# Wide one-hots of the edge counting in a graph network: four tensor_scalar instructions in place of one tensor_tensor

## The chip, the cores and the metric

The kernel runs on one core of a Trainium2 chip. Five engines work side by side: PE (TensorE, matrix products), DVE (VectorE), ACT (ScalarE), POOL (GpSimd) and SP (SyncE, which issues DMAs here). They meet through semaphores. The metric is the device time of one execution in microseconds; lower is better.

## What is computed

Four graph layers over 6250 nodes and 100000 edges (sorted by target node), each with a residual and a layer normalization: attention with 8 heads and a feed-forward part, attention with 4 heads and a gated skip, four rounds of graph convolution, two rounds of sum aggregation with two-layer networks. The two attentions, cut down:

```
score = einsum('ehd,ehd->eh', K[src], Q[dst]) / sqrt(D_HEAD)
s     = exp(clip(score, -5.0, 5.0))[:, :, None]
wV    = segment_sum(V[src] * s, dst);  z = segment_sum(s, dst)         # layer 0
score = einsum('ehc,ehc->eh', q[dst], k[src]) / sqrt(OUT_C)            # layer 1
alpha = softmax of score over the edges of one dst;  out = segment_sum(v[src] * alpha, dst)
```

The later layers need only sums over neighbours. They multiply with a dense matrix of counts, how many edges lead from one node to another, as bytes in device memory. That matrix is made beside the two attentions.

## The kernel before

**The sweeps.** Two sweeps go over the edges in steps of 128 edges, one edge on each partition, all with one target block of 128 nodes. Four steps (HALF = 4) are a half turn; a sweep has 208 half turns. `attend` is the first sweep (layer 0), `score` the second (layer 1).

**POOL** does nothing but gathers in both (`gathers4`, L544): for each step one indirect DMA that fetches keys and values of 128 source nodes. Four to a half turn, 832 to a sweep, into a ring of 8 buffers (`ring4`), each guarded by a semaphore that is waited for before the first gather of a half turn.

**DVE** has the longest list. In a half turn of the first sweep: the message product L788 of the half turn before, then a piece of the counting (`count_lo`, L289, and `count_place`, L295), the product of gathered keys with queries L769 (it waits for the gather), `hits16` L556, the reduction L776, then L781 (clip) and the sums L751 and L321 in turn. In the second: `count_lo`, an L321, `count_place`, L321, `hits16` L556, L321, the product L962 (it waits for the gather), L321 and the reduction L966.

**The counting.** A group is four steps of it. For each step DVE makes two one-hot matrices, both with the edges on the partitions: `by_lo` (128 columns: the source node within its block) and `by_place` (WIDE = 392 columns: source block and place of the target in a window of 8 nodes). PE multiplies them (`count_product`, L331) to a 128x392 block of counts in PSUM, ACT turns it to bytes (`count_move`, L340), DVE adds it to a ring of slots (`count_add`, L321), and SP stores finished slots. The first sweep makes a group in two half turns: a quarter of `by_place` and `by_lo` in the odd one, three quarters in the even one. The second makes one in each half turn and two in 6 of 16 half turns.

The four steps of a group lie innermost in both one-hots: `by_place` is [2, WIDE, HALF], and a source tile `count_fours` of [WIDE, HALF] float16 holds each column's number four times. One tensor_tensor compares it with the four numbers of the group, repeated along the columns. So PE reads the columns of one step 8 bytes apart. `hits16` and `count_lo` use the first 128 columns of `count_fours` in the same way.

DVE's instructions and waits are in the order in which the code writes them; nothing reorders them.

Of the kernel before, what the change touches and what calls it, by code (L numbers as in the profile page):

```python
# [24 lines left out]
P = 128  # L25
# [7 lines left out]
HALF = 4  # L33
# [24 lines left out]
BF16 = mybir.dt.bfloat16  # L58
# [3 lines left out]
F16 = mybir.dt.float16  # L62
# [177 lines left out]
class Counting:  # L240


    def __init__(self, nc, ctx):
        def sb(name, n, dt=F32):
            return ctx.enter_context(nc.sbuf_tensor(name, [P, n], dt))

        def split(t, *shape):
            names = " ".join("abc"[:len(shape)])
            return t[:, :].rearrange(f"p ({names}) -> p {names}", **dict(zip("abc", shape)))

        self.lo, self.place = sb("count_lo", WCOLS, F16), sb("count_place", WCOLS, F16)
        self.tables = sb("count_tables", WCOLS, I32)
        self.fours = split(sb("count_fours", HALF * WIDE, F16), WIDE, HALF)
        self.by_lo = split(sb("by_lo", 2 * HALF * P, BF16), 2, P, HALF)
        self.by_place = split(sb("by_place", 2 * HALF * WIDE, BF16), 2, WIDE, HALF)
# [36 lines left out]
def count_place(dve, ct, c, r, first=0, last=WIDE):  # L292

    n = slice(first, last)
    return dve.tensor_tensor(ct.by_place[:, r % 2, n], ct.fours[:, n], copies(ct.place[:, ds(c * HALF, HALF)], 1, last - first),  # L295
                             ALU.is_equal)
# [28 lines left out]
def count_product(pe, m, ct, c, r, k, bank, banks):  # L325


    if k == 0:
        pe.wait_ge(ct.hot, c + 1)
    wait(pe, ct.moved, c * HALF + k - banks + 1)  # L330
    pe.matmul(m.bank(bank, WIDE), ct.by_lo[:, r % 2, :, k], ct.by_place[:, r % 2, :, k], start=True, stop=True).then_inc(ct.product, 1)  # L331
# [284 lines left out]
def attend(nc, m, ct, adj, table):  # L616
# [4 lines left out]
    with Phase(nc, "at0", "used added hit_ready turned copied q_ready multiplied "  # L621
# [105 lines left out]
        def _(dve):  # L727
# [10 lines left out]
            def half(i, j, h, r, c, first=False):  # L738
# [18 lines left out]
                if odd:  # L757
                    count_lo(dve, ct, c + 1, r // 2 + 1)
                    count_place(dve, ct, c + 1, r // 2 + 1, 0, WIDE // 4)
                    ct.load_of(dve, count_regs[r // 2 % 2], c)  # L760
                    count_stored(dve, ct, c, r // 2)
                else:
                    count_place(dve, ct, c, r // 2, WIDE // 4, WIDE).then_inc(ct.hot, 1)
                    ct.load_to(dve, count_regs[r // 2 % 2], c)
# [30 lines left out]
            count_place(dve, ct, 0, 0, 0, WIDE // 4)  # L795
# [8 lines left out]
            count_place(dve, ct, AT_GROUPS, AT_GROUPS, WIDE // 4, WIDE).then_inc(ct.hot, 1)  # L804
# [1090 lines left out]
def plan_windows(nc, m, ct, t, table):  # L1895


    with Phase(nc, "pw", "rows_in made vec compared counted picked drawn taken loaded0 loaded1 projected copied stored0 stored1") as (
# [48 lines left out]
        def _(dve):  # L1947
# [16 lines left out]
            then(dve.tensor_copy(ct.fours, copies(m.wramp[:, 0:WIDE], 2, HALF)))  # L1964
# [948 lines left out]
```

## Time and profile before

| | |
|---|---|
| median of 3 runs | 5402.13 us |
| lowest, highest | 5399.48, 5411.69 us |
| the profiled execution | 5400.67 us |
| its span, first to last instruction | 5398.3 us |
| mean granted clock of TensorE | 0.885 |
| PE busy | 4350.4 us, 81% |
| DVE busy | 3580.8 us, 66% |
| POOL busy | 2766.0 us, 51% |
| ACT busy | 2266.3 us, 42% |

Busy times are sums over stages that have different limits, so a share of the whole span says little of any one stage. Times in the rows below are microseconds from the start of the span, unless marked as nanoseconds. An instruction of DVE may start some 0.08 us before the recorded end of the one ahead of it, since its start overlaps the other's end.

### The profile page before, as it was taken

How to read it: one execution, taken by the hardware profiler on the slowest of the kernel's cores; microseconds unless marked ns; L12 is line 12 of the kernel's file. 1: busy time of each engine (PE TensorE's matmuls, PEld its weight loads, DVE VectorE, ACT ScalarE, POOL GpSimd, SP SyncE). 2: the span in 40 equal slices, each digit the busy share in tenths (PEclk: the TensorE clock that was granted, in tenths of full speed). 3: DMA queues.
4: the chain of work that ended last, by engine and by line, in shares of the span. 5: the costliest groups of instructions: out<-in, count | busy, mean ns of one | idle time of the engine just before them, and what ended most of it. 6: DMA issues, size and time to landing. Idle time of an engine off the chain costs nothing. (4 is left out here: it accounts for less than half of the span.)

```text
span 5398.3 us, 99723 instructions
## 1 busy us (share of the span) xinstructions
PE 4350.4 (81%) x24072; PEld 3655.1 (68%) x24073; DVE 3580.8 (66%) x7929; ACT 2266.3 (42%) x4134; POOL 2766.0 (51%) x2730
## 2 busy tenths in 40 slices
PE   7566666766767777777468849999999999999998
PEld 4455555554344444444257639999999999999998
DVE  4888888888778888888776674444445654444444
ACT  0333434343245555555246644444444443344333
POOL 0477777774077777777221104444444443344433
PEclk8788888888977787777789959999999999999999
DMA  1444444443267777777235434343444443233332
GB/s 41 124 117 117 118 117 117 116 118 99 96 182 198 200 200 197 203 201 202 70 111 157 136 114 152 132 154 145 149 155 156 174 141 118 96 144 138 133 126 95
DMA packets 543103, 750.01 MB, mean 139 GB/s; under 512 B 57967, under 2 KB 441966, under 8 KB 542734
## 3 DMA queue, kind: packets, MB, share of 16 engines
q1 hardware_dynamic: 461182, 521.35, 28.8%
q0 software_dynamic: 81552, 224.63, 15.5%
q8 instruction: 123, 2.02, 0.1%
q14 instruction: 246, 2.02, 0.1%
HBM read 584.36 MB, written 161.41 MB: 138 GB/s over the span
## 5 line engine op out<-in xcount | busy, mean ns | idle before, releaser
L544 POOL DMA_INDIRECT arena<-table_kv,arena x1664 | 1721.9, 1035 | 653.5 <-issue 506.4
L2350 PE MATMUL ps<-moving,parts 128*128 128x384 f32 (+1 forms) x11662 | 2015.3, 331 | 36.3 <-ACT moving L2412 20.4
L2350 PEld LDWEIGHTS ps<-moving,parts 128*128 128x128 f32 x11662 | 1948.7, 188 | 70.1 <-ACT moving L2412 29.4
L2291 POOL CAST moving<-counts 128x1152 fp32r<-128x1152 uint8 (+1 forms) x420 | 476.7, 1135 | 736.8 <-PE ps L2350 604.7
L340 ACT ACTIVATE counted<-ps 128x392 uint8<-128x392 f32 x1568 | 665.0, 502 | 324.5 <-PE ps L331 283.7
L2291 POOL CAST moving<-big 128x1152 fp32r<-128x1152 uint8 (+1 forms) x413 | 468.4, 1134 | 608.6 <-PE ps L2350 608.6
L331 PE MATMUL ps<-by_place,by_lo 128*128 128x392 bf16 x1568 | 631.3, 525 | 101.9 <-DVE by_place L295 95.5
L654 PE MATMUL ps<-arena 128*128 128x137 f32 x1664 | 325.2, 352 | 338.1 <-DVE arena L788 322.3
L2412 ACT ACTIVATE moving<-counts 128x1152 fp32r<-128x1152 uint8 (+1 forms) x360 | 366.9, 1024 | 436.5 <-PE ps L2350 433.6
L2412 ACT ACTIVATE moving<-big 128x1152 fp32r<-128x1152 uint8 (+1 forms) x354 | 360.4, 1023 | 429.2 <-PE ps L2350 429.0
L654 PEld LDWEIGHTS ps<-arena 128*128 128x128 f32 x1664 | 276.8, 242 | 367.6 <-ACT arena L699 217.6
L2557 DVE CAST moving<-counts 128x1152 fp32r<-128x1152 uint8 (+1 forms) x240 | 312.8, 1303 | 287.2 <-PE ps L2350 287.2
L2557 DVE CAST moving<-big 128x1152 fp32r<-128x1152 uint8 (+1 forms) x236 | 307.5, 1303 | 288.8 <-PE ps L2350 288.8
L562 PEld LDWEIGHTS ps<-arena 128*128 128x128 bf16 x1680 | 141.6, 123 | 523.5 <-DVE arena L556 450.8
L321 DVE TENSOR_TENSOR slots<-slots,counted 128x196 uint16 x1568 | 406.6, 259 | 89.1 <-DVE slots L321 43.0
L562 PE MATMUL ps<-arena 128*128 128x128 bf16 x1680 | 199.6, 252 | 271.5 <-DVE arena L556 269.0
L295 DVE TENSOR_TENSOR by_place<-count_fours,count_place 128x1568 bf16<-128x1568 f16 (+1 forms) x497 | 395.6, 796 | 0.0
L331 PEld LDWEIGHTS ps<-by_place,by_lo 128*128 128x128 bf16 x1568 | 187.7, 123 | 249.2 <-issue 179.2
L883 PE MATMUL ps<-big,arena 128*128 x1672 | 313.5, 348 | 0.4 <-ACT arena L909 0.4
L883 PEld LDWEIGHTS ps<-big,arena 128*128 128x128 f32 x1672 | 292.3, 257 | 27.9 <-issue 18.6
L666 PE MATMUL ps<-big,arena 128*128 x1680 | 288.9, 330 | 0.4 <-ACT arena L694 0.4
L704 ACT ACTIVATE arena<-arena 128x32 f32<-128x32 f32 x208 | 48.3, 232 | 571.5 <-DVE arena L781 571.5
(329 smaller groups left out, 5311.9 us busy)
## 6 DMA issues: line engine op xcount, KB each, us to landing
counts<-adjacency SPq DMA_DIRECT2D x53, 2352.0 KB, 8.6
big<-adjacency SPq DMA_DIRECT2D x52, 2352.0 KB, 8.5
adjacency<-slots SPq DMA_DIRECT2D x784, 98.0 KB
edge_values<-arena SPq DMA_DIRECT2D x208, 256.0 KB, 3.3
arena<-edge_values SPq DMA_DIRECT2D x208, 256.0 KB, 3.2
arena<-table_kv,arena POOLq DMA_INDIRECT x1664
big<-table_norm SPq DMA_DIRECT2D x60, 192.0 KB, 5.6
big<-adjacency SPq DMA_DIRECT2D x7, 1568.0 KB, 6.5
```

What stands on the lines that cost most here:

```text
L295: return dve.tensor_tensor(ct.by_place[:, r % 2, n], ct.fours[:, n], copies(ct.place[:, ds(c * HALF, HALF)], 1, last - first), ALU.is_equal)
L321: dve.tensor_tensor(ct.slot_pairs[:, ds(to[k], WIDE // 2)], ct.slot_pairs[:, ds(of[k], WIDE // 2)], ct.counted_pairs[:, r % 2, k, :], ALU. ...
L331: pe.matmul(m.bank(bank, WIDE), ct.by_lo[:, r % 2, :, k], ct.by_place[:, r % 2, :, k], start=True, stop=True).then_inc(ct.product, 1)
L340: act.activation(ct.counted[:, r % 2, k, :], m.bank(bank, WIDE), ACT.Copy).then_inc(ct.moved, 1)
L544: pool.indirect_dma_start(m.ring4[r][:, k * 2 * D:(k + 1) * 2 * D], None, table, bass.IndirectOffsetOnAxis(m.src[:, j * HALF + k:j * HALF ...
L562: mm = pe.matmul(bank[:, k * P:(k + 1) * P], m.hit16[:, r, :, k], m.ident16, start=True, stop=True)
L654: mm = pe.matmul(summed(k), m.hit[:, r % 2, k, :], m.msg[:, r % 2, k, :], start=True, stop=True)
L883: mm = pe.matmul(m.bank(6 + h)[:, k * P:(k + 1) * P], m.hitT[:, h, k, :], m.q[:, ds(at[k] * D, D)], start=True, stop=True)
L2291: pool.tensor_copy(to, of).then_inc(by_pool, 1)
L2350: mm = pe.matmul(m.bank(g % 2, n * P), d.parts[SOURCE[u]][:, s + q, t_, :], moving[:, q * n * P:(q + 1) * n * P], start=(s + q == 0 and t_ ...
L2412: act.activation(to, of, ACT.Copy).then_inc(by_act, 1)
L2557: dve.tensor_copy(to, of).then_inc(by_dve, 1)
```

## The change

`by_place` is now [2, HALF, WIDE]: a step's 392 columns lie together. It is made a step at a time: a row of the numbers 0 to 391 (`count_iota`, float16) is compared with one number per partition, a tensor_scalar with the operand `ct.place[:, step]`, which is now float32. A group takes four such instructions in place of one (second sweep) or two (first sweep, which now splits them one and three). `count_fours` shrinks to 128 columns. PE reads the columns of a step contiguously.

```diff
-        self.lo, self.place = sb("count_lo", WCOLS, F16), sb("count_place", WCOLS, F16)
+        self.lo, self.place = sb("count_lo", WCOLS, F16), sb("count_place", WCOLS)
-        self.fours = split(sb("count_fours", HALF * WIDE, F16), WIDE, HALF)
+        self.fours = split(sb("count_fours", HALF * P, F16), P, HALF)
+        self.iota = sb("count_iota", WIDE, F16)
-        self.by_place = split(sb("by_place", 2 * HALF * WIDE, BF16), 2, WIDE, HALF)
+        self.by_place = split(sb("by_place", 2 * HALF * WIDE, BF16), 2, HALF, WIDE)
...
-def count_place(dve, ct, c, r, first=0, last=WIDE):
-
-    n = slice(first, last)
-    return dve.tensor_tensor(ct.by_place[:, r % 2, n], ct.fours[:, n], copies(ct.place[:, ds(c * HALF, HALF)], 1, last - first),
-                             ALU.is_equal)
+def count_place(dve, ct, c, r, steps=range(HALF)):
+
+    for k in steps:
+        op = dve.tensor_scalar(ct.by_place[:, r % 2, k, :], ct.iota[:, :], ct.place[:, ds(c * HALF + k, 1)], None, ALU.is_equal)
+    return op
...
-    pe.matmul(m.bank(bank, WIDE), ct.by_lo[:, r % 2, :, k], ct.by_place[:, r % 2, :, k], start=True, stop=True).then_inc(ct.product, 1)
+    pe.matmul(m.bank(bank, WIDE), ct.by_lo[:, r % 2, :, k], ct.by_place[:, r % 2, k, :], start=True, stop=True).then_inc(ct.product, 1)
...
-                    count_place(dve, ct, c + 1, r // 2 + 1, 0, WIDE // 4)
+                    count_place(dve, ct, c + 1, r // 2 + 1, range(1))
...
-                    count_place(dve, ct, c, r // 2, WIDE // 4, WIDE).then_inc(ct.hot, 1)
+                    count_place(dve, ct, c, r // 2, range(1, HALF)).then_inc(ct.hot, 1)
...
-            then(dve.tensor_copy(ct.fours, copies(m.wramp[:, 0:WIDE], 2, HALF)))
+            then(dve.tensor_copy(ct.fours, copies(m.wramp[:, 0:P], 2, HALF)))
+            then(dve.tensor_copy(ct.iota[:, :], m.wramp[:, 0:WIDE]))
```

The order of DVE's instructions in an even half turn of the first sweep, from the message product to the product with the queries; ISA and REGISTER_ALU are the register computations for the operand behind them. Before:

```order
L788 TENSOR_TENSOR arena<-arena 128x4x128
L295 TENSOR_TENSOR by_place<-count_fours,count_place 128x1176
L267 ISA
L267 TENSOR_LOAD count_tables
L275 ISA x2
L769 TENSOR_TENSOR arena<-arena,ps 128x512
```

And after the change, the same place (line numbers are one higher than before):

```order
L789 TENSOR_TENSOR arena<-arena 128x4x128
L296 ISA
L296 TENSOR_SCALAR by_place<-count_iota,count_place 128x392
L296 ISA
L296 TENSOR_SCALAR by_place<-count_iota,count_place 128x392
L296 ISA
L296 TENSOR_SCALAR by_place<-count_iota,count_place 128x392
L268 REGISTER_ALU
L268 TENSOR_LOAD count_tables
L276 ISA x2
L770 TENSOR_TENSOR arena<-arena,ps 128x512
```

One instruction of 1176 elements has become three of 392, right behind the message product; nothing else has moved. In the second sweep, from `count_lo` to the next load of table entries, DVE's order after the change:

```order
L290 TENSOR_TENSOR by_lo<-count_fours,count_lo 128x512
L322 ISA
L322 TENSOR_TENSOR slots<-slots,counted 128x196
L296 ISA
L296 TENSOR_SCALAR by_place<-count_iota,count_place 128x392
L296 ISA
L296 TENSOR_SCALAR by_place<-count_iota,count_place 128x392
L296 ISA
L296 TENSOR_SCALAR by_place<-count_iota,count_place 128x392
L296 ISA
L296 TENSOR_SCALAR by_place<-count_iota,count_place 128x392
L268 REGISTER_ALU
```

Before, one instruction of 128x1568 stood where the four stand.

## Rows read from the trace of the kernel before

**Rows 1.** Busy time by stretch: microseconds, each engine, granted clock, DMA share, GB/s.
```profile
190.00:1320.00 1130.00, 780.12 (x4606) 646.09 (x4605) 976.55 (x2609) 442.62 (x1044) 854.70 (x830) 0.84 0.40 116
1490.00:2620.00 1130.00, 796.85 (x3645) 475.05 (x3643) 928.87 (x2348) 595.27 (x1359) 860.85 (x829) 0.77 0.71 197
3220.00:5398.00 2178.00, 2140.07 (x12603) 2084.79 (x12603) 1037.11 (x1616) 876.40 (x1050) 944.09 (x833) 1.00 0.38 138
```

**Rows 2.** First sweep by shape: busy us, mean ns of one, idle before it.
```profile
L544 POOL DMA_INDIRECT arena<-table_kv,arena x830 | 855.2, 1030 | 252.9 <-issue 252.9
L788 DVE TENSOR_TENSOR arena<-arena 128x512 f32<-128x512 f32 x208 | 143.2, 689 | 0.3 <-ACT arena L704 0.3
L556 DVE TENSOR_TENSOR arena<-count_fours,arena 128x512 bf16<-128x512 f16 x208 | 89.1, 428 | 27.0 <-issue 4.2
L295 DVE TENSOR_TENSOR by_place<-count_fours,count_place 128x1176 bf16<-128x1176 f16 x105 | 80.2, 764 | 0.0
L289 DVE TENSOR_TENSOR by_lo<-count_fours,count_lo 128x512 bf16<-128x512 f16 x104 | 43.5, 418 | 0.0
L295 DVE TENSOR_TENSOR by_place<-count_fours,count_place 128x392 bf16<-128x392 f16 x104 | 37.1, 357 | 0.0
```

**Rows 3.** Second sweep by shape.
```profile
L544 POOL DMA_INDIRECT arena<-table_kv,arena x829 | 861.3, 1039 | 252.6 <-issue 252.6
L331 PE MATMUL ps<-by_place,by_lo 128*128 128x392 bf16 x1149 | 450.4, 527 | 97.8 <-DVE by_place L295 92.0 <-issue 4.2
L321 DVE TENSOR_TENSOR slots<-slots,counted 128x196 uint16 x1152 | 296.1, 257 | 84.4 <-DVE slots L321 42.8 <-issue 20.3 <-ACT counted L340 14.8
L295 DVE TENSOR_TENSOR by_place<-count_fours,count_place 128x1568 bf16<-128x1568 f16 x286 | 277.0, 968 | 0.0
L289 DVE TENSOR_TENSOR by_lo<-count_fours,count_lo 128x512 bf16<-128x512 f16 x286 | 120.5, 421 | 35.0 <-issue 20.5 <-PE ps L331 13.4
L556 DVE TENSOR_TENSOR arena<-count_fours,arena 128x512 bf16<-128x512 f16 x207 | 87.9, 425 | 0.0
```

**Rows 4.** Waits of DVE, first sweep, then second: us, times, longest.
```profile
DVE arena L769 <- DMA arena<-table_kv,arena: 101.9, 180, 1.5
...
DVE arena L962 <- DMA arena<-table_kv,arena: 75.2, 59, 5.2
```

**Rows 5.** Durations of the gathers, second sweep, shortest, median, longest.
```profile
L544 POOL DMA_INDIRECT arena<-table_kv,arena x829: 942/947/2379, 1489.5 to 2602.2; - x166
```

**Rows 6.** Timeline of the second sweep: a gather behind L295.
```profile
2012.93 0.97 DVE L295 TENSOR_TENSOR by_place<-count_fours,count_place 128x1568 bf16<-128x1568 f16 x1
2013.12 1.59 POOL L544 DMA_INDIRECT arena<-table_kv,arena  x1 [0.30 <-issue]
```

**Rows 7.** Timeline of the first sweep: a gather behind L788.
```profile
709.78 0.69 DVE L788 TENSOR_TENSOR arena<-arena 128x512 f32<-128x512 f32 x1
710.06 1.23 POOL L544 DMA_INDIRECT arena<-table_kv,arena  x1 [0.30 <-issue]
710.39 0.42 DVE L289 TENSOR_TENSOR by_lo<-count_fours,count_lo 128x512 bf16<-128x512 f16 x1
```

**Rows 8.** Timeline of the first sweep: L781 in a gather; then all L781.
```profile
707.56 0.94 POOL L544 DMA_INDIRECT arena<-table_kv,arena  x1 [0.30 <-issue]
708.19 0.32 DVE L781 TENSOR_SCALAR arena<-arena 128x32 f32<-128x32 f32 x1
...
L781 DVE TENSOR_SCALAR arena<-arena x208: 167/175/386, 197.7 to 1302.0; 128x32 f32<-128x32 f32 x104
```

**Rows 9.** Timeline of the planning: DVE instructions with a number per partition.
```profile
10.10 1.28 DVE L472 TENSOR_SCALAR arena<-arena,small 128x896 f32<-128x896 f32 x2
...
26.54 0.28 DVE L482 TENSOR_SCALAR arena<-arena,tile_id 128x128 f32<-128x128 f32 x1
26.74 0.28 DVE L484 TENSOR_SCALAR arena<-arena,tile_id 128x128 f32<-128x128 f32 x1
```

**Rows 10.** Costliest groups of the page: the dense part's product.
```profile
L2350 PE MATMUL ps<-moving,parts 128*128 128x384 f32 (+1 forms) x11662 | 2015.3, 331 | 36.3 <-ACT moving L2412 20.4
```

More of the change, by code:

```diff
@@ L794, in _ @@
             count_lo(dve, ct, 0, 0)
-            count_place(dve, ct, 0, 0, 0, WIDE // 4)
+            count_place(dve, ct, 0, 0, range(1))
             dve.memset(m.sums[:, 0:BLOCKS * A0], 0.0).then_inc(ones_in, 1)
@@ L803, in _ @@
                     half(i, RINGS * i + r, r % 2, r, RINGS // 2 * i + r // 2)
-            count_place(dve, ct, AT_GROUPS, AT_GROUPS, WIDE // 4, WIDE).then_inc(ct.hot, 1)
+            count_place(dve, ct, AT_GROUPS, AT_GROUPS, range(1, HALF)).then_inc(ct.hot, 1)
             to_count, of_count = ct.at(dve, count_regs[(AT_GROUPS - 1) % 2])
```

## The prediction

> **What bounds the kernel now.** I read the windows first [rows 1]. The program has three long stretches: the first sweep (190 to 1320 us), the second (1490 to 2620 us) and the dense part after 3220 us. The last has PE busy 2140 of 2178 us and runs none of the changed code, so the question lies in the two sweeps. In neither is PE, ACT or DVE full: DVE is busy 977 and 929 of 1130 us.
>
> The groups of each sweep by shape [rows 2, 3] settle it. POOL issues 4 indirect gathers a half turn, 832 in a sweep. Its only idle time in either sweep is "issue", 252.9 and 252.6 us, 0.305 us ahead of each gather: it never waits for a ring buffer, for DVE or for a transfer. 855.2 + 252.9 = 1108 us is the first sweep, 861.3 + 252.6 = 1114 us the second. DVE waits for what POOL fetched, 101.9 us at L769 in the first and 75.2 us at L962 in the second [rows 4]. So **a sweep lasts as long as POOL's gathers, and DVE has 102 and 75 us to spare**. A change on DVE counts by what it does to the time of a gather, until DVE has used its slack up.
>
> Next, what makes a gather long. The shortest is 942 ns and the median 947, but the longest 2379 [rows 5] and the means are 1030 and 1039 [rows 2, 3]. Against 0.944 us each the excess is 855.2 - 830 x 0.944 = 71.7 us in the first sweep and 861.3 - 829 x 0.944 = 78.7 us in the second. The timeline shows the cause. In [rows 6] L295 runs from 2012.93 to 2013.90; the gather that starts at 2013.12 takes 1.59 us and ends 0.81 us after L295. In [rows 7] L788 ends at 710.47 and the gather ends at 711.29, 0.82 us later. An undisturbed gather needs 0.944 us, so both look as if they had started 0.13 us ahead of the end of the DVE instruction. Both DVE instructions read two tensors in SBUF. **First hold:** a gather that starts while such an instruction runs waits for it, to 0.13 us before its recorded end.
>
> The other direction is in [rows 8]. L781, a tensor_scalar with one SBUF source, starts 0.63 us into a gather and ends with it, at 708.51, in place of taking its median 175 ns: it got going at +0.78 us. Its longest is 386 ns, 0.21 above the median, so it is held from +0.57 us at the latest. **Second hold:** from +0.57 to +0.78 us a gather keeps a tensor_scalar of this sort waiting. Nothing here shows whether a tensor_scalar that is already running makes the gather wait at +0.57; L781, with 32 elements, is too short.
>
> **The change, part by part.** L295 goes, by_place is filled by tensor_scalar of 392 elements, four in a group. 104 or 105 groups are made in the first sweep, 286 in the second.
>
> *Length of one new instruction.* L482 and L484, also with a number per partition, start 0.195 us apart at 128 float32 elements and last 0.28; two L472 of 896 take 1.28 us, which with the same overlap of 0.08 is 0.60 apart [rows 9]. That is 0.53 ns an element and 0.13 us fixed. The new source and result are 2 bytes wide. No row has a one-source instruction of that kind, but two-source ones show what width does: L788, 512 float32, 689 ns; L289, 512 of 2 bytes, 418 ns [rows 2]: 0.53 ns an element less, half the rate of 1.06. I take the same halving: 392 x 0.265 + 0.13 = 0.23 us apart, 0.315 long. If the width bought nothing it is 392 x 0.53 + 0.13 = 0.34; at one element a cycle, as L788, 0.54.
>
> *DVE's work.* Second sweep: L295 took 0.968 - 0.08 = 0.885 us of DVE's time, four new ones take 0.93: +0.04 x 286 = +12 us. First sweep: 0.68 + 0.27 = 0.95 a group before, 0.93 after: nothing. Each new instruction has a register computation of its own ahead of it (the rows of the order above), 4 where there was 1; short beside 0.23, and I cost it at nothing.
>
> The Trainium skill (VectorE: DVE Perf Modes, section "The perf-mode tier table") lets tensor_scalar on 2-byte SBUF operands stream at four elements a cycle, tensor_tensor at two. The halving above agrees with it. By that rule alone a group would stream 1568 elements in 0.41 us in place of 0.82, and DVE would win 117 us in the second sweep; by the rows three more fixed parts of 0.13 us take all of that back.
>
> *DVE held by POOL.* The four run 0.93 us and are held if one wants to start in the second hold, 0.21 us in each 1.31 us: chance (0.93 + 0.21) / 1.31 = 0.87, mean wait half of 0.21: 0.09 x 286 = 26 us in the second sweep and 10 in the first. Together +38 of the 75 us of slack in the second; the first has 102.
>
> *POOL, first hold, second sweep.* A hold of length h hits starts in proportion to h and then costs h/2, so shares go by h squared, h being the duration less 0.13 us: L295 0.84^2 x 286 = 202, L289 24, L556 18, L321 19, in all 263. L295's share of 78.7 us is 60 us. The new ones: 0.185^2 x 1144 = 39, that is 12 us. This is the gain: -48 us.
> *Second hold, second sweep.* If a running tensor_scalar delays POOL at +0.57 as it does at the start, another 12 us; if it keeps POOL to its recorded end, 0.315^2 x 1144 = 114 or 34 us; if not at all, 0. I take 18, between the first two. **Second sweep: -60 + 12 + 18 = -30 us, bounds -48 and -14.** DVE allows 75 - 38 = 37 us of it, so it is barely covered, and -37 is the most unless DVE's own waits shrink. They may, a little: the 392-column product has mean 527 ns with columns 8 bytes apart, against 331 for 384 columns at L2350 [rows 3, 10]; its columns now lie together. That is not counted.
>
> *First sweep.* By the same squares L295 would own 48 of 140, 24 us. But it stands right behind L788, on which the gather waits first; the next starts 1.25 us later, when L295 is over. I take 5 of the 24; 2 come back from the new ones. New is this: after L788 ends at E, the gather's second hold falls at E + 0.44. In even half turns three new instructions start at E - 0.08, + 0.15 and + 0.38; the third would hold to E + 0.565. 104 x 0.125 = 13 us if POOL waits for it; to its recorded end, with the one of odd half turns too, 40; 0 if not at all. **First sweep: -5 + 2 + 13 = +10 us, bounds -17 and +37.**
>
> *Preparation.* One copy shrinks by 1056 elements and one of 392 is added, once: under 1 us.
>
> Sum: -30 + 10 = **-20 us**. The profiled execution took 5400.67 us, span 5398.3, 1.5 us under the median of 5402.13. 5400.67 - 20 = 5380.7; I say **5381 us**.
>
> **The rivals.**
> *A, the pair stays locked (slower).* If back-to-back tensor_scalars never let POOL in between, each group holds as one block of 3 x 0.23 + 0.185 = 0.88 us: 65 us at the first hold and 65 at the second, +70 in the second sweep; in the first, +25. 5400.67 + 95 = **5496 us**. It decides from the point where more than two in a row keep the hold. Against it: in [rows 7] L289 stood ready behind L788, started at 710.39 before L788's end, and POOL still got in at L788's end. For it: those only read through the contested side, and a tensor_scalar may also take the writing side. The Trainium skill (SBUF — State Buffer, section "SBUF: two separate sides") warns that a Vector instruction in a two-port mode keeps GpSimd from writing its descriptors, with tensor_copy as the example; L781's row agrees that the two exclude each other, in the opposite order. 10 in 100.
> *B, the width buys nothing (slower).* 0.34 us apart: 1.34 a group, +0.45 x 286 = +130 us in the second sweep, plus 26 held, against 75 of slack: +81. The first sweep absorbs 0.19 x 208 = 40. DVE becomes the bound of the second sweep: **5480 us**. 8 in 100, with the one-element rate (5700 us and more) in it.
> *C, nothing to see.* The two holds give back what the one took; the gathers keep their mean of 1.03 to 1.04: **5401 us**. 17 in 100.
> *D, the second hold never waits for DVE.* -48, capped by DVE at about -40 with faster products, and -3 in the first sweep: **5358 us**. 20 in 100.
> The forecast has the remaining 45.
>
> **The numbers.** Forecast and own range: 5381, 5350 to 5405. A measurement tells 0.2%, 11 us, from no change. Faster: all of D and three quarters of the forecast, with a little of C, 0.56. Same: most of C and a tenth of the forecast, 0.20. Slower: A, B, and the sixth of the forecast in which the first sweep goes to its upper bound, 0.24. The range that leaves out 2 in 10 runs from 5345 to 5450; A and B lie beyond.
>
> **What the profile would show.** Right: L296 at about 0.315 us, starts 0.23 apart; L544 still with "issue" as its only idle time, its mean down to about 1.00 in the second sweep and up to 1.04 in the first; the wait at L962 down to some 10 us. Wrong: L296 at 0.42 or more (B); L544 above 1.08 (A); a sweep in which DVE no longer waits for gathers, where POOL's gain is lost.

## The result, and the profile after

| | before | after |
|---|---|---|
| median | 5406.55 us | 5418.13 us |
| lowest, highest (20 executions each) | 5395.16, 5415.69 | 5407.31, 5424.99 |
| the profiled execution | 5400.67 us | 5417.27 us |
| its span | 5398.3 us | 5415.2 us |

The ratio is 1.0021, 95% interval 1.0014 to 1.0028: **slower by 0.2%**, 12 us, where 20 us less was forecast. It is a small number, but the experiments below show that it is the difference of two larger ones. (The changed kernel was measured once more with the first experiments, as twice_after, and stood 18 us above the kernel before beside it.)

The windows of the kernel after, columns as in [rows 1]:

```profile
190.00:1320.00 1130.00, 732.96 (x4613) 639.50 (x4614) 979.71 (x2825) 442.77 (x1045) 850.31 (x828) 0.84 0.41 116
1490.00:2620.00 1130.00, 676.00 (x3595) 485.96 (x3596) 940.60 (x3161) 583.88 (x1334) 805.61 (x825) 0.75 0.70 195
3220.00:5398.00 2178.00, 2135.78 (x12569) 2081.32 (x12569) 1040.18 (x1625) 878.10 (x1050) 946.85 (x833) 0.99 0.38 140
```

In the second sweep POOL's busy time fell from 861 to 806 us in the same 1130 us, and yet it issued 825 gathers in place of 829. Something else now sets the pace. The granted clock of TensorE there is 0.75 after 0.77, and PE is busy 676 of 1130 us: it bounds nothing. The groups of that sweep by shape, columns as in [rows 3]:

```profile
L545 POOL DMA_INDIRECT arena<-table_kv,arena x825 | 805.6, 977 | 296.8 <-issue 238.5 <-SPq L859 58.3
L332 PE MATMUL ps<-by_place,by_lo 128*128 128x392 bf16 x1128 | 315.9, 416 | 114.2 <-DVE by_place L296 112.3 <-issue 0.6
L296 DVE TENSOR_SCALAR by_place<-count_iota,count_place 128x392 bf16<-128x392 f16 x1132 | 298.0, 324 | 0.0
L322 DVE TENSOR_TENSOR slots<-slots,counted 128x196 uint16 x1130 | 291.1, 258 | 141.2 <-issue 63.1 <-DVE slots L322 38.9 <-ACT counted L341 36.1
L963 DVE TENSOR_TENSOR arena<-arena,ps 128x512 f32<-128x512 f32 x206 | 140.4, 682 | 11.4 <-DMA arena<-table_kv,arena 7.9 <-issue 1.7 <-PE ps L884 1.4
L290 DVE TENSOR_TENSOR by_lo<-count_fours,count_lo 128x512 bf16<-128x512 f16 x282 | 118.6, 421 | 34.7 <-issue 31.6 <-PE ps L332 1.2
```

A gather takes 977 ns, not 1039. But POOL, which never waited before, now waits 58.3 us. Its releaser is SP's L859, the line after which a ring buffer is free; the buffer is full of rows that DVE has not yet used, since DVE's own wait for gathers has shrunk from 75.2 to 7.9 us (L963). **DVE has become the bound of the second sweep.** And it has done so less by working than by standing still: ahead of L322 it is idle 141.2 us, of which "issue" is 63.1. It was 84.4 with 20.3.

From its first gather to its last L322 (L321 before) the second sweep took 1485.5 to 2618.3 before, 1132.8 us, and takes 1481.1 to 2635.6 after, 1154.5 us: **+21.7**. The first sweep is 2.4 us shorter, and its two groups are unchanged in what they say, with POOL idle for "issue" alone and DVE still with time to spare:

```profile
L545 POOL DMA_INDIRECT arena<-table_kv,arena x828 | 850.9, 1028 | 252.4 <-issue 252.4
L770 DVE TENSOR_TENSOR arena<-arena,ps 128x512 f32<-128x512 f32 x208 | 143.1, 688 | 102.5 <-DMA arena<-table_kv,arena 102.4
L296 DVE TENSOR_SCALAR by_place<-count_iota,count_place 128x392 bf16<-128x392 f16 x419 | 134.7, 364 | 0.0
```

Where does DVE stand idle in the second sweep? The timeline of DVE shows one half turn (start and duration in us, in brackets the idle time ahead and its cause):

```profile
1997.08 1.04 DVE L296 TENSOR_SCALAR by_place<-count_iota,count_place 128x392 bf16<-128x392 f16 x4
1998.17 0.26 DVE L322 TENSOR_TENSOR slots<-slots,counted 128x196 uint16 x1
1998.35 0.43 DVE L557 TENSOR_TENSOR arena<-count_fours,arena 128x512 bf16<-128x512 f16 x1
1999.32 0.26 DVE L322 TENSOR_TENSOR slots<-slots,counted 128x196 uint16 x1 [0.54 <-issue]
```

The gap lies between `hits16` (L557) and the next `count_add`; over the sweep it has a mean of 0.46 us, and had 0.18 before (worked out from the starts in the two traces). In the code `ct.load_of` stands at that place: DVE's sequencer loads four slot numbers from a table in SBUF into registers (L272). The L322 behind it doesn't use them. They go into the set `following` and are used by the next group's L322. But it stands behind the load in DVE's list, and after this load the L322 starts 0.23 us or more after the load's end, in every half turn of the trace after. Three views of single lines show what the sequencers did at this moment (min/median/max ns, then the times; DVEq and SPq are the sequencers of DVE and SP):

```profile
L347 SPq TENSOR_LOAD <-count_tables x1: 300/300/300, 1998.0 to 1998.0; - x1
L348 SPq TENSOR_LOAD <-count_tables x1: 626/626/626, 1998.4 to 1998.4; - x1
L272 DVEq TENSOR_LOAD <-count_tables x1: 611/611/611, 1998.5 to 1998.5; - x1
```

SP loads its own table entries for `count_store` (L347, L348), and its second load overlaps DVE's. The first of SP's two takes 0.30 us; here the second and DVE's both take over 0.61. Over the sweep, the kernel after first, then the kernel before:

```profile
L272 DVEq TENSOR_LOAD <-count_tables x283: 337/510/944, 1490.4 to 2618.6; - x142
```

```profile
L271 DVEq TENSOR_LOAD <-count_tables x287: 336/345/876, 1494.8 to 2616.0; - x144
```

The median load of DVE went from 345 to 510 ns. Counting overlaps in the trace, 38 of 283 loads met one of SP's before and 170 of 278 after (mean 0.62 us for those, 0.40 for the rest). It is SP's second load that goes with the long ones: of the 160 loads L272 that met L348, 130 took 0.5 us or more, and of the other 128 of the sweep 19; the 15 beside L347 alone have a median of 345 ns. An overlap doesn't explain every long load, though: in the kernel before, SP's second load met no load of DVE's 207 times and still took 0.5 us or more in 101 of them. So two causes stood to be told apart: the load *starts* late, since the four L296 each bring a register computation of 57 ns to the same sequencer, or the load *takes* long, since it now meets SP's.

### The profile page after: what moved, and what is told of

The parts are those of the page before. It is cut to its first block and busy times, and to the rows that moved or that the text cites. A ratio compares the mean times of both kernels' runs of the same rounds, so it can differ in the third digit from the quotient of the medians.

```text
span 5415.2 us, 100831 instructions
## 1 busy us (share of the span) xinstructions
PE 4189.2 (77%) x24072; PEld 3665.1 (68%) x24073; DVE 3607.2 (67%) x9001; ACT 2264.6 (42%) x4134; POOL 2714.0 (50%) x2730
## 5 line engine op out<-in xcount | busy, mean ns | idle before, releaser
L545 POOL DMA_INDIRECT arena<-table_kv,arena x1664 | 1667.3, 1002 | 698.8 <-issue 493.6
L2414 ACT ACTIVATE moving<-big 128x1152 fp32r<-128x1152 uint8 (+1 forms) x354 | 360.3, 1023 | 430.6 <-PE ps L2352 430.4
L332 PE MATMUL ps<-by_place,by_lo 128*128 128x392 bf16 x1568 | 441.8, 404 | 123.9 <-DVE by_place L296 121.9
L322 DVE TENSOR_TENSOR slots<-slots,counted 128x196 uint16 x1568 | 406.5, 259 | 148.0 <-issue 63.1
L296 DVE TENSOR_SCALAR by_place<-count_iota,count_place 128x392 bf16<-128x392 f16 x1568 | 437.3, 335 | 0.0
L884 PE MATMUL ps<-big,arena 128*128 x1672 | 331.4, 362 | 0.4 <-ACT arena L910 0.4
L884 PEld LDWEIGHTS ps<-big,arena 128*128 128x128 f32 x1672 | 305.5, 269 | 6.5 <-issue 2.9
L667 PE MATMUL ps<-big,arena 128*128 x1680 | 292.0, 332 | 0.4 <-ACT arena L695 0.4
```

What stands on the lines that cost most here:

```text
L296: op = dve.tensor_scalar(ct.by_place[:, r % 2, k, :], ct.iota[:, :], ct.place[:, ds(c * HALF + k, 1)], None, ALU.is_equal)
L322: dve.tensor_tensor(ct.slot_pairs[:, ds(to[k], WIDE // 2)], ct.slot_pairs[:, ds(of[k], WIDE // 2)], ct.counted_pairs[:, r % 2, k, :], ALU. ...
L545: pool.indirect_dma_start(m.ring4[r][:, k * 2 * D:(k + 1) * 2 * D], None, table, bass.IndirectOffsetOnAxis(m.src[:, j * HALF + k:j * HALF ...
L884: mm = pe.matmul(m.bank(6 + h)[:, k * P:(k + 1) * P], m.hitT[:, h, k, :], m.q[:, ds(at[k] * D, D)], start=True, stop=True)
L2414: act.activation(to, of, ACT.Copy).then_inc(by_act, 1)
```

## The experiments

The theory at the start: **T** (theory S in the expectations), POOL's side went as forecast or better, and DVE lost the gain at the uncovered load. Rivals: **R1**, the gathers cost DVE more than they did (second hold), and **R2**, four short instructions are simply more work for DVE (R1 and R2 together are theory W); **P**, the chain from the product through ACT to L322 sets the pace. **R3** was formed after these: the load is late by the register computations alone, or long by a collision with SP (theory C). Ratios are to the kernel before, measured beside each (medians 5398.25 with late_after, late_before, twice_after and four_tt; 5402.08 with split_after, one_ts, static_after and late_four_tt; 5395.76 with the three that move SP's loads). In two kernels, one_ts and static_after, part of the one-hots is replaced as told there; the counts are then other ones, the program takes a long branch behind the dense part that the others don't (13388.32 and 13384.19 us in all), and only their sweeps are read.

**late_after.** The load moves to a place where DVE's engine has 0.68 us of work in hand:

```diff
                     hits16(dve, m, ct, (r + 2) % 4, (j + 2) * HALF).then_inc(hit_ready, 1)
-                    ct.load_of(dve, following, c)
                     count(2)
...
                                       m.bank(6 + r % 2).rearrange("p (k n) -> p k n", k=HALF), ALU.mult).then_inc(multiplied, 1)
+                    ct.load_of(dve, following, c)
                     count(3)
```

> The changed kernel, with the second sweep's load of the four source offsets (L272) moved from behind hits16 (L557) to behind the product L963, ahead of the last L322. Theory S (the sequencer of DVE): after the change DVE's queue is filled with short instructions, its sequencer runs less far ahead, and the load stands uncovered between L557 and the next L322 (idle 0.46 us a single group against 0.18 before). Behind a product of 0.6 us it is covered again: that idle falls to 0.2 us or less, about 0.25 us x 206 = 50 us come free on DVE, POOL becomes the bound of the second sweep again at (0.98 + 0.305) x 832 = 1070 us, DVE waits for gathers at L963 again, and the kernel is some 35 to 50 us faster than the changed one: 5365 to 5385 us. Theory W (DVE's added work and its being held by POOL fill the sweep, wherever the load stands): nothing or under 10 us is gained, the idle time turns up at another instruction. Theory P (the chain from product to ACT to L322 sets the pace): the same as W, with L322 waiting for ACT.

5352.17 us, ratio 0.9906 (0.9891 to 0.9921). The changed kernel measured beside it (twice_after, below) took 5416.68, so the move is worth 64 us; the second sweep is 64.3 us shorter (1090.2). That is more than the 35 to 50 expected. The groups of its second sweep:

```profile
L545 POOL DMA_INDIRECT arena<-table_kv,arena x823 | 802.6, 975 | 250.8 <-issue 247.4 <-SPq L859 3.4
L322 DVE TENSOR_TENSOR slots<-slots,counted 128x196 uint16 x1149 | 295.0, 257 | 94.8 <-DVE slots L322 39.5 <-issue 38.8 <-ACT counted L341 8.4
L962 DVE TENSOR_TENSOR arena<-arena,ps 128x512 f32<-128x512 f32 x207 | 140.4, 678 | 12.6 <-DMA arena<-table_kv,arena 11.3 <-issue 1.1
```

and its DVE timeline, where the gap behind L557 is gone and 0.17 us are left behind the product:

```profile
2003.77 0.25 DVE L322 TENSOR_TENSOR slots<-slots,counted 128x196 uint16 x1
2003.94 0.41 DVE L557 TENSOR_TENSOR arena<-count_fours,arena 128x512 bf16<-128x512 f16 x1
2004.47 0.26 DVE L322 TENSOR_TENSOR slots<-slots,counted 128x196 uint16 x1
2004.65 0.68 DVE L962 TENSOR_TENSOR arena<-arena,ps 128x512 f32<-128x512 f32 x1
2005.50 0.26 DVE L322 TENSOR_TENSOR slots<-slots,counted 128x196 uint16 x1 [0.17 <-issue]
```

POOL's mean is the same 975 as with the change alone (977), its wait for the ring is gone, and the time with it. T holds. R1, R2 and P fall as the main cause: the edit touches neither DVE's work nor the order of the chain through ACT, the gathers are as long as with the change, and the time came back.

**late_before.** The same move in the kernel before.

> The kernel before with the same load moved in the same way. Theory S: before the change POOL bounds the second sweep, so DVE's time is free and nothing moves: within 0.2% of before (5400 to 5412 us), gathers with mean 1.03 to 1.05 us. If the load's place by itself were worth the time whatever the counting does, this kernel would gain as many microseconds as the changed one gains from it.

5384.5 us, ratio 0.9965 (0.9952 to 0.9978). A small gain where none was expected: POOL never waited there, but its gathers went from 1039 to 1023 ns. The groups of its second sweep:

```profile
L544 POOL DMA_INDIRECT arena<-table_kv,arena x829 | 847.7, 1023 | 252.7 <-issue 252.4 <-SPq L858 0.3
L321 DVE TENSOR_TENSOR slots<-slots,counted 128x196 uint16 x1152 | 294.0, 255 | 71.9 <-DVE slots L321 39.5 <-issue 13.3 <-ACT counted L340 8.1
```

That what DVE does earlier or later shifts which of its two-source instructions a gather meets is a guess that no run tests. Against the same kernel before, the change alone gives +18 us (twice_after) and the move alone -14, and together they give -46: the move is worth 14 us without the change and 64 with it.

**twice_after.** A second, identical `ct.load_of` behind the first, to double the suspected cost.

> The changed kernel with the load L272 issued twice in each single group of the second sweep (the same values into the same registers). Theory S: the load is on DVE's path there, so a second one costs nearly all its length, 0.35 to 0.5 us x 206 = 70 to 105 us: 5490 to 5525 us. Theories W and P: it is hidden behind the waits that are there anyhow, under 20 us.

5416.68 us, 1.0028 (1.0019 to 1.0038). The trace has 392 loads L272, as the trace of the change has, not more: the build merged the two, and this is the changed kernel once more. It tells nothing of the theory; it repeats the measurement of the change, beside late_after.

**split_after.** The doubling done in a way that the build keeps:

```diff
-                    ct.load_of(dve, following, c)
+                    dve.load(following[HALF:HALF + 2], ct.tables[32:33, ds(c * HALF, 2)])
+                    dve.load(following[HALF + 2:], ct.tables[32:33, ds(c * HALF + 2, 2)])
```

> The changed kernel with the load L272 of each single group in the second sweep cut in two loads of two values each, at the same place, behind hits16 (L557). It is the real form of the doubled load: two identical loads were merged into one when the kernel was built, so that run was the changed kernel again. Theory S (the load stands uncovered on DVE's sequencer ahead of an L322): the idle time ahead of that L322 grows from 0.46 us by nearly a load, 0.35 us or more, a single group takes 4.6 us or more in place of 4.29, and the second sweep is 55 to 100 us longer than the changed kernel's: 5470 to 5515 us. Theories W and P (work and holds, or the product chain, set the pace): under 20 us.

5603.21 us, 1.0374 (1.036 to 1.0387): in the expected direction and twice as far (187 us in the second sweep, where 55 to 100 was expected). The second sweep takes 1341.8 us. Its groups by shape, and then the two loads by their lines:

```profile
L545 POOL DMA_INDIRECT arena<-table_kv,arena x731 | 700.0, 958 | 430.9 <-SPq L859 245.0 <-issue 185.9
L322 DVE TENSOR_TENSOR slots<-slots,counted 128x196 uint16 x970 | 249.1, 257 | 281.6 <-issue 227.2 <-DVE slots L322 39.1 <-ACT counted L341 14.4
```

```profile
L958 DVEq TENSOR_LOAD <-count_tables x176: 528/959/1142, 1492.2 to 2615.6; - x176
L959 DVEq TENSOR_LOAD <-count_tables x176: 524/528/1172, 1492.8 to 2616.6; - x176
```

Two loads of two values are far dearer than one of four: at least 0.52 us each, with a median of 0.96 for the first. POOL's gathers are the shortest of all (958), and it waits 245 us. DVE's sequencer alone can make the sweep 18% longer than before (1341.8 / 1132.8).

**four_tt.** The other way round: the kernel before with `count_place` of the second sweep in four tensor_tensors of 392, without the change's layout.

```diff
-                    count_place(dve, ct, c + 1, p + 1).then_inc(ct.hot, 1)
+                    for n4 in range(4):
+                        placed = count_place(dve, ct, c + 1, p + 1, n4 * (WIDE // 4), (n4 + 1) * (WIDE // 4))
+                    placed.then_inc(ct.hot, 1)
```

> The kernel before with the second sweep's wide compare cut in four tensor_tensor instructions of 392 elements, one behind the other; the kind of instruction, the layout and PE's strided columns stay as before. If it is the length of one uninterrupted instruction that makes gathers long (first hold), the gathers of the second sweep fall from a mean of 1.039 to about 0.98 to 1.00 us, as with the change, though these are the same two-tensor instructions. If it is their kind or their sum of busy time, the mean stays at 1.03 or above. For the time: four instructions stand 0.27 us apart, 1.10 us a group against 0.89, 60 us more work for DVE, and by theory S the loads lose their cover too: slower than before by 30 to 90 us (5435 to 5495 us). By theory W alone (work minus the 75 us of slack) about 5400 to 5410 us.

5408.3 us, 1.0015 (1.0005 to 1.0024). The groups of its second sweep:

```profile
L544 POOL DMA_INDIRECT arena<-table_kv,arena x828 | 831.1, 1004 | 264.6 <-issue 246.3 <-SPq L858 18.3
L321 DVE TENSOR_TENSOR slots<-slots,counted 128x196 uint16 x1140 | 292.1, 256 | 98.7 <-DVE slots L321 37.6 <-issue 29.2 <-ACT counted L340 28.6
```

By theory S 5435 to 5495 us was expected here, by theory W 5400 to 5410: the time came out as W says, so this run by itself speaks for the rival. It shows how much of the picture comes from the cutting alone: gathers down from 1039 to 1004 of the change's 977, the wait for the ring begun (18.3 us), the median load up to 469 ns. But the load is not late: it starts 0.61 us ahead of the end of `hits16` (medians here and below, from the traces), against 0.53 in the kernel before and 0.37 in the kernel after. four_tt has one register computation a group. The rest of the change's picture goes with the kind of the instruction, the four computations and the layout together; no run separates the kind from the layout.

**late_four_tt.** four_tt with the load moved.

> The kernel before with the second sweep's compare in four tensor_tensor instructions and the load moved behind the product. It has both parts of the moved changed kernel (short holds, covered load) but not the kind of instruction nor the contiguous columns. Theory: POOL bounds the sweep again, gathers of mean 1.00 as without the move, (1.00 + 0.305) x 832 = 1086 us against 1118 before: 25 to 35 us faster than before, 5365 to 5380 us, 10 to 25 us behind the moved changed kernel, since its DVE has 0.13 us a group more work and its gathers wait a little longer. If the kind or the layout matters by itself, it stays near before, 5390 us or more.

5395.95 us, 0.9989 (0.9981 to 0.9998), where 5365 to 5380 was expected. The ring's wait went (3.0 us), but the gathers went back to 1034 ns, the longest to 2848 ns: POOL is the bound again, with DVE waiting 39.6 us for it. late_after, with tensor_scalars and the new layout, keeps them at 975. So cutting and a covered load are not enough for its gain; whether the kind of the instruction or the layout gives the rest was not tried apart.

**static_after.** The number per partition is always that of the first group, at a fixed place, so that DVE's sequencer has nothing to compute. The one-hots of all later groups are thus left out.

```diff
-        op = dve.tensor_scalar(ct.by_place[:, r % 2, k, :], ct.iota[:, :], ct.place[:, ds(c * HALF + k, 1)], None, ALU.is_equal)
+        op = dve.tensor_scalar(ct.by_place[:, r % 2, k, :], ct.iota[:, :], ct.place[:, k:k + 1], None, ALU.is_equal)
```

> The changed kernel with the number per partition read at a fixed place, the first four columns, in all groups: no register computation stands ahead of any tensor_scalar. The output is not the reference's: every group's wide one-hots are those of the first four steps. If it is the register computations (four where there was one) that put the sequencer behind, the idle ahead of L322 falls from 0.46 to about 0.2 us and the kernel gains 30 to 60 us on the changed one: 5360 to 5385 us. If it is that short instructions fill the queue, so that the sequencer can stand only two of them ahead of the engine, nothing changes: 5410 to 5420 us. I hold the second for likelier, since the four tensor_tensor version, too, had 0.29 us of idle there.

The second sweep takes 1083.6 us (1478.9 to 2562.5), 71 less than with the change, with the load where the change left it. Its groups by shape:

```profile
L545 POOL DMA_INDIRECT arena<-table_kv,arena x824 | 802.2, 974 | 251.1 <-issue 246.8 <-SPq L859 4.3
L322 DVE TENSOR_TENSOR slots<-slots,counted 128x196 uint16 x1149 | 294.1, 256 | 77.7 <-DVE slots L322 40.6 <-ACT counted L341 21.8 <-issue 8.3
```

and DVE's load by its line, min/median/max:

```profile
L272 DVEq TENSOR_LOAD <-count_tables x286: 335/344/907, 1493.3 to 2560.2; - x143
```

"issue" ahead of L322 falls to 8.3 us and the load to 344 ns; it starts 0.63 us ahead of the end of `hits16` in place of 0.37. So the four register computations are needed for the loss, though the other outcome was held for likelier. It is not that the loads now miss SP's: 182 of 287 overlap one, more than with the change. But most of these, 132, meet SP's first load, or its first and the start of its second, and keep a median of 344 to 345 ns; of the 50 beside the second alone, 7 in 10 take 0.5 us or more. The earlier start moves DVE's load away from SP's second.

**one_ts.** The four instructions merged into one tensor_scalar of 1568 elements with the first step's number (the one-hots of the other three steps are left out): one register computation, and a single long instruction.

> The changed kernel with the tensor_scalars of a count_place merged: one instruction over 4 x 392 elements (3 x 392 and 392 in the first sweep), all compared with the number of the group's first step. The output is not the reference's: three of four steps get the wrong one-hots. It has the rate, the layout and the kind of the change with the number of instructions of before. At 0.265 ns an element it is 0.415 + 0.21 = 0.63 us long, 0.55 apart, 0.38 us a group less DVE work than the change. Theory S: one long instruction covers what the sequencer does next as L295 did, the idle ahead of L322 behind L557 falls back to about 0.2 us, POOL bounds the second sweep: with first holds of 0.5^2 x 286 = 72 against 202 of before its gathers have a mean of 1.00 and the kernel takes 5355 to 5380 us. If a running tensor_scalar also kept POOL waiting at the second hold, gathers of 1.15 us and more would appear that do not start under a two-tensor instruction, and the mean would be above 1.02. If the idle ahead of L322 stays at 0.46 with the shorter work, theory S is wrong on what gives cover, though the time may still fall.

The second sweep takes 1089.3 us (1481.8 to 2571.1), 65 less than with the change. Its tensor_scalar by its line, and its gathers by shape:

```profile
L296 DVE TENSOR_SCALAR by_place<-count_iota,count_place x286: 614/622/786, 1490.6 to 2566.1; 128x1568 bf16<-128x1568 f16 x143
```

```profile
L545 POOL DMA_INDIRECT arena<-table_kv,arena x826 | 815.1, 987 | 251.7 <-issue 248.3 <-SPq L859 3.3
```

One of 1568 takes 622 ns, one of 392 takes 316 (medians, the second of the kernel after): (622 - 316) / 1176 = 0.26 ns an element. And a tensor_scalar of 0.62 us leaves the gathers at 987 ns, where the tensor_tensor of 0.97 us had them at 1039. But what theory S expected of the cover did not come: the idle time behind `hits16` is 0.39 us a group, against 0.46 with the change and 0.2 expected, and the load starts only 0.30 us ahead of the end of `hits16`, although there is one register computation. A compare of 0.62 us in all, in place of 1.04, gives less cover too. This kernel gains by having less work for DVE, 0.38 us in each of 286 groups, so it can't say which of work and sequencer was decisive in the change; static_after, with the full work, does.

**sp_early_after.** SP's part alone. SP's two loads move ahead of its wait for the gathered rows, where they run early; DVE's program is that of the change, to the instruction.

```diff
                 first = isinstance(j, int) and j == 0
+                if not first:
+                    count_store_regs(sp, ct, regs, groups[0][0] - 1)
                 sp.wait_ge(gathered[q], before + 64 * filled + 64)
```

> The changed kernel with SP's two table loads for a group of the second sweep (L347, L348) moved ahead of SP's wait for the gather and its store of the edge values; DVE's program is untouched. In the changed kernel 170 of 278 loads L272 of DVE overlap one of these loads of SP in time and then take 0.62 us on average, against 0.40 for the others; before the change 38 of 283 did. Theory C (collision): once SP no longer waits for gathers, its loads follow DVE's last L322 at a fixed distance and meet L272; moved 0.6 us and more ahead they no longer do, L272 falls to a median of 0.35 us, the idle ahead of L322 from 0.46 to about 0.25 us, 0.2 x 206 = 40 us come free: 5370 to 5385 us, and POOL is the bound again. Theory S alone (the sequencer is late because of the four register computations, whatever SP does): under 10 us, 5408 to 5420 us.

5368.65 us, 0.9938 (0.9921 to 0.9956): 27 us below the kernel before, where the change was 12 to 18 above. The second sweep takes 1111.4 us (1478.8 to 2590.2). Its groups by shape:

```profile
L551 POOL DMA_INDIRECT arena<-table_kv,arena x824 | 802.0, 973 | 258.8 <-issue 246.3 <-SPq L867 12.5
L322 DVE TENSOR_TENSOR slots<-slots,counted 128x196 uint16 x1149 | 295.4, 257 | 100.9 <-DVE slots L322 41.9 <-issue 33.4 <-ACT counted L341 17.9
```

and the load by its line:

```profile
L272 DVEq TENSOR_LOAD <-count_tables x286: 336/343/699, 1493.3 to 2587.9; - x143
```

The median load is back at 343 ns, the "issue" wait at 33.4 us, and 43 of the second sweep's 71 us (to static_after) are back. **Most of the loss hangs on when SP makes its loads.** DVE's load still starts late, 0.32 us ahead of the end of `hits16`; that the other 28 us are the price of this later start is the reading that is left, not a run of its own. What exactly makes the two loads long when they meet stays open: here SP's second load overlaps DVE's other load (L268) 216 times, and only in 32 of them does DVE's take 0.5 us or more.

**sp_early_before** and **late_sp_early.** The same move of SP's loads in the kernel before, and together with DVE's moved load in the kernel after.

> The kernel before with SP's loads moved in the same way. POOL bounds its second sweep and DVE has 75 us of slack: by both theories no more than some 10 us, 5390 to 5410 us.

> The changed kernel with both moves, DVE's load behind the product and SP's loads early. Both theories: POOL already bounds the second sweep with the first move alone (gathers 0.975 us, no wait), so the second move can give only what it changes in the phase between DVE and POOL: within 10 us of the 5352 us of the first move alone.

5409.09 us, 1.0016 (1.0006 to 1.0026), and 5349.44 us, 0.9905 (0.9889 to 0.9921). Before the change the place of SP's loads cost no time, and moving them only shifts the gathers a little the wrong way (1052 ns). With DVE's load already covered, SP's placement adds nothing to late_after's 0.9906.

The second sweeps side by side, first gather to last L322 or L321:

| kernel | second sweep, us | mean gather, ns | POOL waits for the ring, us | DVE's load, median ns | "issue" ahead of L322, us |
|---|---|---|---|---|---|
| before | 1132.8 | 1039 | 0 | 345 | 20.3 |
| after | 1154.5 | 977 | 58.3 | 510 | 63.1 |
| static_after | 1083.6 | 974 | 4.3 | 344 | 8.3 |
| one_ts | 1089.3 | 987 | 3.3 | 344 | 46.9 |
| late_after | 1090.2 | 975 | 3.4 | 365 | 38.8 |
| sp_early_after | 1111.4 | 973 | 12.5 | 343 | 33.4 |
| four_tt | 1143.1 | 1004 | 18.3 | 469 | 29.2 |
| late_before | 1119.4 | 1023 | 0.3 | 345 | 13.3 |

## Why the prediction was wrong

**Length of a new instruction: right.** Predicted 0.315 us long and 0.23 apart; the median is 316 ns, and the four take 1.04 us in the timeline above, 0.316 + 3 x 0.24. The halving by width, worked out as 0.265 ns an element, measured 0.26. The Trainium skill (VectorE: DVE Perf Modes, section "The perf-mode tier table") puts tensor_scalar on 2-byte operands in SBUF at four elements a cycle, and this length agrees. B is out.

**POOL, first hold: right in mechanism, a little larger.** The excess over 0.944 us fell from 78.7 to 805.6 - 825 x 0.944 = 26.8 us, by 52. The squares gave -48, without a second hold. No gather of the second sweep is longer than 1220 ns; the longest was 2379. That a gather which starts under a tensor_scalar waits for it, as the squares assume, one_ts shows: 119 gathers that started with 0.15 to 0.55 us of it left, and under no two-source instruction, ended 0.82 us after its end (median).

**POOL, second hold: 18 us priced, none there.** The timeline of the first sweep has the arrangement that the prediction feared, three L296 behind the message product (L789):

```profile
699.42 0.68 DVE L789 TENSOR_TENSOR arena<-arena 128x512 f32<-128x512 f32 x1
699.69 1.24 POOL L545 DMA_INDIRECT arena<-table_kv,arena  x1 [0.30 <-issue]
700.02 0.98 DVE L296 TENSOR_SCALAR by_place<-count_iota,count_place 128x392 bf16<-128x392 f16 x3
```

The gather ends at 700.93, which is L789's end at 700.10 plus 0.83: the first hold and nothing more. The three L296 take 0.98 in place of 3 x 0.23 + 0.08 = 0.77 us: it is DVE that was held. The third of them took 524 ns, 0.21 more than the median. Over the first sweep L296 has a mean of 364 ns against a median of 316, and POOL's mean is 1028 after 1030. And of the gathers that met no such instruction at their start but one at +0.57 us, 10 here and 12 in one_ts, none took more than 950 ns. Rival D's mechanism was the right one. A is out. The first sweep came out at -2.4 us, not +10.

**DVE's work and holds: about right.** Busy time per second sweep rose from 928.87 x 1132.8 / 1130 = 931 to 940.60 x 1154.5 / 1130 = 961 us: +30, where 12 + 26 = 38 was said.

**The step that failed: "Each new instruction has a register computation of its own ahead of it (...), 4 where there was 1; short beside 0.23, and I cost it at nothing."** That computation is no work of the engine, and the engine did run on under it. But the sequencer that makes it also has to get through the load ahead of the next L322. With one computation, or with none, the sequencer was 0.53 to 0.63 us ahead of the end of `hits16` when it came to the load (before, four_tt, static_after); with four it was 0.37 ahead. The prediction took DVE's slack, 75 us less 38, and asked only what its *instructions* would add; the cover of the load at L271 was never costed. In place of nothing the step was worth 71 us of the second sweep (static_after). The prediction did name a sweep in which DVE no longer waits for gathers as its sign of being wrong, and that sign came, but it had no price for it. The sum for DVE in the second sweep, all per sweep: +30 busy, idle ahead of L322 from 84.6 to 141.2 x 1154.5 / 1130 = 144.3, +60, and L290's idle the same. That is +90 against 75.2 us of slack that DVE had. Some 8 of it stayed as DMA waits, and 90 - 75 + 8 = 23, against the +21.7 measured. This is bookkeeping of one trace against the other; the causes rest on the experiments.

**What made it dear was another queue.** The second half of the failed step is SP, which the prediction left out because the change does not touch it. SP makes its two loads behind its wait for a half turn's gathers. While POOL was the bound SP's second load fell on DVE's other load instead (L267, 73 times). In 54 of them DVE's took 0.5 us or more, but it ended at least 0.37 us before the long L295 did, and the L321 behind started without a gap. With the gathers early and DVE the bound, 160 fell on L272, which stood uncovered. That DVE, later still, then kept the bound, and why the loads fall just there, is read from the order of the code and was not tried by itself. What it costs was: sp_early_after takes just SP's timing away and gains 43 us in the sweep; static_after lets DVE's load start earlier and gains 71; late_after covers the load and gains 64.

**The outcome beside the cases.** D's 5358 us, 43 below its base, is about what the change gives once the load is covered: 5352.17, 46 below the kernel before beside it. The result lies in none of the four rivals: its mechanism, DVE's sequencer, was not among them. The only slow rivals were a locked pair and a dead width; a rival of the kind "DVE uses up its slack in waits of its own" would have decided from 45 us on, which is 0.16 us in each of 286 groups.

**What stays open.** Why the move of the load is worth 14 us in the kernel before, and why late_four_tt's gathers are back at 1034 ns: neither is explained. What makes a sequencer's load take 0.6 us in place of 0.3, as SP's second load often does with no load of DVE's beside it, and why two short loads in a row take 0.53 us and more each, was not followed up, nor was the gain from PE's contiguous columns taken by itself.

**A version that beats both** came out of it: the change with the load behind the product (late_after), 0.9906 of the kernel before (0.9891 to 0.9921).

## What to carry to other kernels

When one long instruction becomes several short ones, cost the sequencer as well as the engine: count the register computations and the loads that the sequencer must get through, and look at the first instruction behind each load. Here it waited for the load though it does not use what is loaded, and it was the length of the old instruction that covered it. A slack read from a wait is spent by idle time as well as by work, so list the places where an engine is idle for "issue" before counting on it. And when a change can move the bound from one engine to another, ask of each queue that it doesn't touch what it was waiting for: it will keep another time afterwards, and may fall on the very resource that has become short. A load whose values are used much later can stand anywhere before that: moving it behind a long instruction costs one line and was worth 64 us here.

## What the runs showed of the hardware

- A sequencer's load of four values from SBUF into registers had a median of 0.30 us on SP for the first of two in a row and 0.34 on DVE (before). Where DVE's L272 and SP's second load overlapped by more than 0.2 us (121 times, after), their medians were 0.68 and 0.65 us; an overlap with SP's first load left DVE's at 0.345. SP's second load had a median of 0.47 us where it met no load of DVE's (207 times, before). Two loads of two values behind each other took at least 0.52 us each (split_after).
- The instruction behind such a load started 0.23 us or more after the load's end, although it did not use the loaded values (L322 behind L272, after).
- A gather held DVE's tensor_scalar (by 0.21 us, the third of those at 700.02), while a running tensor_scalar, of 0.32 us or of 0.62, was not seen to hold a gather at its second hold (22 cases). A gather that started under the one of 0.62 us ended 0.82 us after it.
- A tensor_scalar with a number per partition, float16 to bfloat16: 316 ns for 392 elements and 622 for 1568.
- A product of 392 bfloat16 columns had a mean of 416 ns (shortest 328, median 353) when they lie together, and 527 (shortest 505) when they lie 8 bytes apart [rows 3], at a granted clock of 0.75 and 0.77.
